# Queries and keys in three parts through the scratch, read in one or two transfers, with new first loads and new orders

## What is computed

```
Q = layernorm(x) @ Wq + bq                 # 8 x 128 x 512
K = context @ Wk + bk                      # 8 x 128 x 128
V = context @ Wv + bv
w = softmax(Q K^T / 4)                     # per head, 4 query heads share a key head
x = x + tanh(g_xattn) * ((w V) @ Wo + bo)
n = layernorm(x)
h = silu(n @ w1^T) * (n @ w3^T)            # 1792 features, block scales on w1, w3, w2
x = x + tanh(g_ffn) * (h @ w2^T)
```

## Time and profile before

| | |
|---|---|
| median of 3 runs | 391.2 us (389.21 to 392.38) |
| the profiled execution | 391.0 us, of which the span is 389.3 |
| TensorE busy | 371.2 us (95%) |
| VectorE, ScalarE, GpSimd busy | 253.6, 184.7, 154.9 us |
| moved by transfers | 34.96 MB, mean 90 GB/s |
| read from and written to device memory | 26.04 MB, 7.34 MB |

### The profile page before, as it was taken

One profiled execution on the slowest core, in us unless ns is written; L12 is line 12 of the kernel. 1 busy time (PEld: TensorE's weight loads), 2 busy tenths in 40 slices (PEclk: granted clock), 3 DMA queues, 4 the chain that ended last, 5 costly groups with the idle time before them and its releaser, 6 DMA issues.

```text
span 389.3 us, 6031 instructions
## 1 busy us (share of the span) xinstructions
PE 371.2 (95%) x2216; PEld 303.8 (78%) x2216; DVE 253.6 (65%) x411; ACT 184.7 (47%) x322; POOL 154.9 (40%) x134
## 2 busy tenths in 40 slices
PE   8979699989899999889999999999999999999996
PEld 6868589888677778668888888888888888888885
DVE  4666389979899976875767777443954344544434
ACT  3562389878889983622332422332332332432320
POOL 7534469989989987733333443000000000000000
PEclk9998699999999999989999999999999999999999
DMA  8979855767543500890000000000200000000002
GB/s 287 252 239 240 263 121 137 215 167 229 123 97 97 175 2 2 327 400 2 0 0 0 0 0 0 1 0 0 109 1 0 0 0 0 0 0 0 0 0 108
DMA packets 15604, 34.96 MB, mean 90 GB/s; under 512 B 2176, under 2 KB 7296, under 8 KB 14784
## 3 DMA queue, kind: packets, MB, share of 16 engines
q1 hardware_dynamic: 14864, 33.65, 28.9%
q10 hardware_dynamic: 720, 1.05, 0.8%
HBM read 26.04 MB, written 7.34 MB: 86 GB/s over the span
## 4 chain that ended last, share of the span: by engine, by line
PE 56%; DVE 1%; issue 0%
PE ps L1866 19%; PE ps L1868 19%; PE ps L1867 18%; DVE X L1317 1%; DVE hL L1339 0%
## 5 line engine op out<-in xcount | busy, mean ns | idle before, releaser
L1866 PE MATMUL ps<-x2HL,w13H 128*128 128x512 f32 x224 | 89.1, 398 | 0.0
L1868 PE MATMUL ps<-x2HL,w13L 128*128 128x512 f32 x224 | 88.5, 395 | 0.0
L1867 PE MATMUL ps<-x2HL,w13H 128*128 128x512 f32 x224 | 88.4, 394 | 0.0
L483 POOL TENSOR_TENSOR PL<-E,PH 128x512 f16<-128x512 f32 x64 | 74.1, 1178 | 10.2 <-ACT PH L784 7.9
L494 POOL TENSOR_TENSOR wres<-wres,gsc 128x1536 f32<-128x1536 f32 x14 | 42.0, 3006 | 48.7 <-DVE hf L1330 48.7
L803 ACT ACTIVATE T<-ps 128x512 f32<-128x512 f32 x28 | 16.7, 596 | 79.4 <-PE ps L1868 79.4
L1868 PEld LDWEIGHTS ps<-x2HL,w13L 128*128 128x128 f32 x224 | 42.0, 187 | 10.4
L1867 PEld LDWEIGHTS ps<-x2HL,w13H 128*128 128x128 f32 x224 | 42.0, 187 | 9.8
L1866 PEld LDWEIGHTS ps<-x2HL,w13H 128*128 128x128 f32 x224 | 42.0, 188 | 9.7
L1323 DVE SCALAR_TENSOR_TENSOR A<-T,ps 128x512 f32<-128x512 f32 x28 | 19.2, 685 | 46.0 <-ACT T L803 46.0
L1866 PE MATMUL ps<-w2H,hH 128*128 128x512 f32 x112 | 44.9, 401 | 2.7 <-DVE x2HL L1306 2.7
(11 more groups left out here) (102 smaller groups left out, 647.2 us busy)
## 6 DMA issues: line engine op xcount, KB each, us to landing
wres<-in_wff SPq DMA_DIRECT2D x14, 768.0 KB, 7.2
Qst<-qscr SPq DMA_DIRECT2D x21, 256.0 KB, 4.5
X<-in_x SPq DMA_DIRECT2D x8, 256.0 KB, 6.1
ct<-in_ctxt SPq DMA_DIRECT2D x6, 256.0 KB, 7.8
x2HL<-kscr SPq DMA_DIRECT2D x24, 64.0 KB, 3.5
qscr<-QTH SPq DMA_DIRECT2D x3, 512.0 KB, 4.3
qscr<-QTL SPq DMA_DIRECT2D x3, 512.0 KB, 3.7
out<-X SPq DMA_DIRECT2D x6, 256.0 KB, 2.1
```

Of the source, the lines that this page charges most:

```text
L483: pool.tensor_tensor(PL[:, g % NL, :], E[:, g % NE, :], PH[:, g, :], ALU.subtract).then_inc(pL_ok, 1)
L1866: pe.matmul(out_ap, aH, bH, start=start, stop=False)
L1867: pe.matmul(out_ap, aH, bL, start=False, stop=False)
L1868: return pe.matmul(out_ap, aL, bH, start=False, stop=stop)
```

## The change

It has five parts.

1. The scratch tensors get a third part. The query scratch holds high, high, low (parts 0, 1, 2), the key scratch high, low, high, just as the rows are stacked. So each pair writes queries three times and keys three times; the queries of a block come back in one read of 96 rows, the keys of a pair in two reads of 48 rows (every second row of 96). The order of features in the weights (`queries`, `keys`) is changed to match. A read waits for all three writes.
2. First loads: all are issued by SP, in the order key weights, context 0 and 1, x 0 and 1, value weights, biases, context 2, x 2, context 3, first half of the query weights. TensorE begins with keys and values in place of x. The select reads move behind the first queries, the out weights (1 MB) ahead of them.
3. `NWARM` is 12.
4. Some small work changes engine: the high half of the second query weights from VectorE to ScalarE, the first V part of all four pairs and the second of two pairs from ScalarE to VectorE, the first `clear_keys` from GpSimd to VectorE, one `max_rows` and two `q_high` from VectorE to ScalarE, two `shift` and two `shift2` from GpSimd to VectorE, one `epsilon2` the other way.
5. The lists of all engines are in a new order.

```
-NWARM = 16
+NWARM = 12
...
-        qscr = nc.dram_tensor("qscr", [NBATCH // 2, 2, 2, P, GJ * P], F32).ap()
-        kscr = nc.dram_tensor("kscr", [NBATCH // 2, 2, P, TWO], F32).ap()
+        qscr = nc.dram_tensor("qscr", [NBATCH // 2, 2, 3, P, GJ * P], F32).ap()
+        kscr = nc.dram_tensor("kscr", [NBATCH // 2, 3, P, TWO], F32).ap()
...
-        def keys_out(eng, p, low):
-            eng.dma_start(kscr[p, low], r32((KTL if low else KTH)[:])).then_inc((kh_out, kl_out)[low], 16)
-
-        def keys_in(eng, p, t, gg):
+        def keys_out(eng, p, t):
+            eng.dma_start(kscr[p, t], r32((KTL if t == 1 else KTH)[:])).then_inc((kh_out, kl_out, kg_out)[t], 16)
+
+        def keys_in(eng, p, gg):
             s = (NBATCH - NKST + 2 * p % NKST) * P
-            r = 32 * t + DH * gg
-            eng.dma_start(r32(kall(r, r + DH)[:, gg:KVH:2, s:s + TWO]),
-                         kscr[p, t % 2, 64 * gg:64 * gg + 64].rearrange("(r h) n -> r h n", h=PAIRS)).then_inc((k_in0, k_in1)[p % 2], 16)
+            eng.dma_start(r32(x2HL[gg:ROWS:2].rearrange("p a k n -> p (a k) n")[:, gg:KVH:2, s:s + TWO]),
+                         kscr[p].rearrange("t (d g h) n -> g (t d) h n", g=2, h=PAIRS)[gg]).then_inc((k_in0, k_in1)[p % 2], 16)
...
-        def queries_in(eng, n, t, done):
-            eng.dma_start(r32(Qst[32 * t:32 * t + 32, slot(n), :, :]).rearrange("r h n -> r (h n)"),
-                         qscr[n // 2, t // 2, n % 2].rearrange("(r h) n -> r (h n)", h=PAIRS)).then_inc(done, 16)
+        def queries_in(eng, n, done):
+            eng.dma_start(r32(Qst[0:ROWS, slot(n), :, :]).rearrange("r h n -> r (h n)"),
+                         qscr[n // 2, n % 2].rearrange("t (r h) n -> (t r) (h n)", h=PAIRS)).then_inc(done, 16)
...
+            sp.wait_ge(qg_out, 32)
+            sp.wait_ge(qh_out, 32)
+            sp.wait_ge(ql_out, 32)
+            queries_in(sp, 2, q_in0)
...
-            pe.wait_ge(k_in1, 96)
-            pe.wait_ge(q_in0, 48)
+            pe.wait_ge(k_in1, 32)
+            pe.wait_ge(q_in0, 16)
             scores(2, 0)
```

More of the change, by code:

```diff
@@ L351, in _ @@
             keys_out(sp, 2, 0)
-            sp.wait_ge(mrows, 2)
+            out_bias_in(sp)
+            queries_in(sp, 1, q_in2)
+            sp.wait_ge(sel_ok, 3)
+            select_rows(sp, 0)
+            select_rows(sp, 1)
+            keys_out(sp, 2, 2)
+            select_rows(sp, 2)
+            tokens_in(sp, 7)
+            select_rows(sp, 3)
+            sp.wait_ge(mrows, 1)
+            max_in(sp, 0, 0, 2)
+            sp.wait_ge(mrows, 2)
+            max_in(sp, 0, 2, 4)
+            sp.wait_ge(qT_H, 8)
@@ new lines, in _ @@
+            sp.wait_ge(qT_L, 12)
+            queries_out(sp, 2, 2, 0, 4, ql_out)
+            sp.wait_ge(mrows, 4)
+            max_in(sp, 2, 0, 4)
+            queries_out(sp, 2, 0, 0, 4, qh_out)
+            keys_out(sp, 3, 2)
+            sp.wait_ge(st_ps, 16)
+            keys_in(sp, 2, 1)
+            keys_in(sp, 2, 0)
+            sp.wait_ge(qg_out, 48)
+            sp.wait_ge(qh_out, 48)
+            sp.wait_ge(ql_out, 48)
+            queries_in(sp, 4, q_in2)
+            keys_out(sp, 3, 0)
@@ L1390, in _ @@
-            mean(3)
+            dve.wait_ge(vt_ps, 2)
+            v_first(2, W0)
+            dve.wait_ge(v1_ok, 2)
+            v_residue(2, W0)
             dve.wait_ge(qT_H, 3)
             q_low(W2, 2)
-            dve.wait_ge(mean1, 4)
+            statistics(5)
             epsilon(3)
-            v_residue(2, W0)
+            mean(4)
+            dve.wait_ge(qT_H, 4)
+            q_low(W1, 3)
+            v_third(2, W0)
             dve.wait_ge(rs1_ok, 4)
             shift(3)
-            dve.wait_ge(qT_H, 4)
@@ L1429, in _ @@
-            max_high(0, 2)
-            mean(5)
             dve.wait_ge(qT_H, 6)
-            q_low(W2, 1)
+            q_low(W0, 1)
             dve.wait_ge(s_ps, 4)
@@ L1480, in _ @@
             denominators(1)
+            mean(7)
             dve.wait_ge(den_ok, 2)
             sums(1)
-            dve.wait_ge(kT_H, 4)
-            k_low(W0)
+            dve.wait_ge(mean1, 8)
+            epsilon(7)
             dve.wait_ge(sum_ok, 2)
@@ L1524, in _ @@
             row_max(3, 0)
+            dve.wait_ge(den_ok, 5)
+            sums(0)
+            dve.wait_ge(xTH_ok, 7)
+            x_low(6, W2)
+            dve.wait_ge(sum_ok, 5)
+            divide(0)
+            dve.wait_ge(s_ps, 14)
+            row_max(3, 1)
             dve.wait_ge(pv_ps, 12)
@@ L2182, in _ @@
             scores_t(2, 4)
-            project_q(W2, 1, 0, 2)
+            project_q(W0, 1, 0, 2)
+            pe.wait_ge(k_in0, 64)
+            pe.wait_ge(max_ok, 16)
+            pe.wait_ge(q_in2, 32)
+            scores(4, 0)
             pe.wait_ge(E_ok, 20)
@@ L2266, in _ @@
             scores_t(4, 0)
+            pe.wait_ge(max_ok, 22)
+            scores(5, 2)
+            project(W2, DM, aTH, aTL, O0, 1)
+            pe.wait_ge(E_ok, 32)
+            scores_t(4, 1)
             pe.wait_ge(pL_ok, 29)
@@ L2301, in _ @@
-            pe.wait_ge(k_in1, 192)
-            pe.wait_ge(max_ok, 24)
-            pe.wait_ge(q_in1, 144)
-            scores(6, 0)
-            pe.wait_ge(mL_ok, 6)
-            turn_max(W1, 0, 4)
+            pe.wait_ge(E_ok, 37)
+            scores_t(4, 6)
+            turn4(W2, ON).then_inc(aT_ps, 1)
+            pe.wait_ge(max_ok, 25)
+            scores(6, 1)
+            pe.wait_ge(PH_ok, 38)
+            scores_t(4, 7)
+            pe.wait_ge(pL_ok, 35)
             pe.wait_ge(on_ok, 17)
@@ L2352, in _ @@
             turn_max(W2, 0, 4)
+            pe.wait_ge(on_ok, 19)
+            values(4, 6)
             pe.wait_ge(E_ok, 44)
             scores_t(5, 5)
+            values(4, 7)
+            turn4(W1, x2n).then_inc(x2T_ps, 1)
+            pe.wait_ge(max_ok, 29)
+            scores(7, 1)
+            pe.wait_ge(E_ok, 45)
+            scores_t(5, 6)
             pe.wait_ge(on_ok, 20)
             values(5, 0)
+            pe.wait_ge(pL_ok, 42)
             values(5, 1)
-            pe.wait_ge(mrows, 7)
```

1694 lines of the change are left out of this document (812 added, 882 removed).

## The result

The changed kernel takes 395.5 us (median of 20 runs, 390.3 to 400.4), the kernel before 391.7 beside it; the ratio is 1.009, with a 95% interval of 1.005 to 1.013. Forecast were 385 us and faster. In two later jobs (a job is one session on one chip, with the kernels in turn) the same changed kernel stood at 1.0114 (1.0035 to 1.0193; median 398.1) and 1.0188 (1.0136 to 1.0240; median 397.6) of the kernel before. Medians are over all executions; the ratios leave out those more than 1.5% above the fastest of their kernel, and the one profiled with the first measurement was such a one.

A forecast was written before the change was run, and what follows sets the result against it. The prediction took the first stage to hang on the DMA transfers, not on TensorE. Its terms, 3.4 + 1.3 + 1.5 = 6.2 us, taken from 391.1 gave 384.9, say 385 us, with a range of 380 to 394.

The forecast's parts named there:

- First term: First stage, up to the scores of block 2: gain of 3.4 us (3.0 + 1.4 - 1.0), from 0 to 6.
- the DMA work is through at 52.2: First stage: 2.1 us net transfer cost, less 1.95 us of idle time gone, after 52 us; landing at 54.0.
- The DMA share in 20 to 30: Sign of being right: the DMA engines' share in 20 to 30 us rises from 0.75 to 0.9.
- The scores of block 2 behind 57 us: Sign of being wrong: these scores start after 57 us, where 53 to 55 was forecast and 56.96 measured before.
- The wait at the door: Sign of being right: TensorE's wait before the feed-forward, 2.74 us at 166.94, falls below 2 us.
- price of an 8 KB packet: Sign of being right: 8 KB packets still cost 0.5 to 0.6 us of DMA engine time each.
- Second term: Key waits before the scores of blocks 4 and 6, 1.1 and 1.6 us: half gained, 1.3 us (0 to 2.7).
- Third term: Door of the feed-forward: a third of 4.4 us of wait and slow clock gained, 1.5 us (-1 to 4.4).
- work moved between engines: Mostly before 50 us: adds no instruction in sum; some 1 us for the largest piece if the cover fails.
- The transfers take it back: Rival, first stage: idle time stays 3.9 us, key packets 0.086; 388 to 390 us, within 1%; chance 0.28.
- One read waits for three writes: Rival, reads for blocks 4 and 6: TensorE stands 4 us or more at each; about 396 us; chance 0.14.
- port rule: Rival: each query read takes 1.2 us less, 3.6 us before block 2's scores; about 381 us; chance 0.08.

The follow-up runs named there:

- kernel with the queries first: Changed kernel, with second half of pair 1's queries and block 2's maxima transposes ahead of block 1's scores: 393.0 us (1.0039), again 394.9 us (1.0138).

## Why the prediction was wrong

**First term, 3.4 us of gain; measured a loss of about 1** (the table's 1.8 less the 0.9 of the warm-up). The step that failed is "so the DMA work is through at 52.2 [...] the scores of block 2 now start there, by waiting". The bill of the packets was right: I had 48.4 us of engine time before those scores. The windows give 0.89 x 20 + 9.9 + 10.7 + 6.3 = 44.7 up to 52, and the read of block 2, which hadn't begun, adds 96 packets of 8 KB at 0.54, 3.2 us: 47.9. But the engines' idle time didn't halve, from 3.9 to 1.95. It is 52 - 44.7 = 7.3 us, of which the first 2.5 us hold 2.0 (1.8 before), so it grew to 5.3; 3.7 of them lie in 42 to 52, most of it in 42 to 47, where SP waits for the second piece of the maxima and has the writes of pair 1's queries behind that. I read that all engines are full and took their sum for the bound. They are full up to about 43 us; from there the bound is the chain read, scores of block 1, second half of the queries of pair 1, write, read. And the kernel before reached these scores without a wait, so to start them by waiting at 54.0, with 1.4 us more done, TensorE had to save 4.4 us of what it lost before them. My sum had no term for that, and the waits ahead of blocks 0 and 1 went from 5.13 to 6.08 us. The rows for it were in front of me: the order in which these stand, and 3.38 us of wait ahead of block 1 in the earlier trace rows. The kernel with the queries first shows the chain: read and scores of block 2 move up by 4.6 and 2.5 us, no byte less moved.

**The signs.** The DMA share in 20 to 30 rose to 0.99, as said, and proved nothing, since it had only moved. The scores of block 2 behind 57 us was my sign of being wrong, and it came (59.39); the other, a wait for queries of 3 us or more at blocks 4 and 6, didn't (2.07 and none). The wait at the door (1.38 us) and the price of an 8 KB packet (0.50 us) were as said.

**Second term, 1.3 us, was right in its size and wrong in its sum.** Key waits fell from 2.7 us to 1.5. But a wait for queries of 2.07 us stands ahead of block 4, which the kernel before had for keys with 1.1. From 60 to 120 us the middle lost 2.3 more, it gained nothing: the waits for keys and queries went from 2.7 us to 3.6, and the mean clock from 1.00 to 0.94.

**Third term, 1.5 us: the gain is there, larger than I put it (lost in 160 to 190: 4.7 to 2.2), and the step that failed lies beside it.** I wrote that the new order "puts that scaling elsewhere" and didn't ask what else it puts elsewhere. The first product of the feed-forward had moved up, ahead of the values of block 6, and with it the same kind of VectorE operation into a run of GpSimd. It stood for 4.70 us. The stretch of 120 to 160 lost 5.5 us more, the largest piece of the miss, and my sum didn't have it at all: I costed "work moved between engines" only up to 50 us. That operation's place is shown to be only about 1 us of it (8.1 us lost, 6.9 with the product and the operation moved back); what takes the rest stays open.

**The rivals.** "The transfers take it back" came nearest in the first stage, for the wrong reason: idle time didn't stay at 3.9 us, it grew, and key packets did become cheaper. "One read waits for three writes" ended on the right side, but the three writes cost nothing in the old orders, and its sum was off: 11 us for 2.7 on 391.1, less the third term's 1.5, is 398, not 396. The gain of the port rule didn't come: three reads of 32 rows in 60 to 64 us gave 0.54 us a packet; in the changed kernel the window 60 to 64 holds one read of 96 rows.

```profile
DMA packets 93, 0.61 MB, mean 153 GB/s; under 512 B 14, under 2 KB 14, under 8 KB 20
...
q1 hardware_dynamic: 93, 0.61, 61.6%
```

61.6% of 64 us is 39.4; less about 1 us for the small ones and 6 packets of weights at some 0.3, 36.6 over 73 packets of 8 KB is 0.50 us each. By the rule of the Trainium skill ("SBUF — State Buffer", section on the DMA port swizzle), as I estimated from it, the wider read would have cost two thirds of the price, 0.36. It costs nine tenths. That doesn't refute the rule: the estimate took the three reads of 32 rows for served one after another, and they were issued within 1.25 us (from 59.78) and took 4.4 us each to land, so they may have overlapped. Key reads over 48 rows did become cheaper: in 101 to 104 us (second window below) 54.0% of 48 us is 25.9, less 23 packets of 8 KB at 0.54 leaves 13.5 over 208, 0.065 us each, where I had bounds of 0.086 and 0.047.

```profile
DMA packets 231, 0.39 MB, mean 128 GB/s; under 512 B 16, under 2 KB 208, under 8 KB 208
...
q1 hardware_dynamic: 231, 0.39, 54.0%
```

## What to carry to other kernels

When most engines are nearly full, don't take the sum of their work for the bound of a stage: write down the chain of issue, landing, product and next issue, and ask for each moved instruction what stands behind it in its queue. When a change brings a new order for every engine, go through the new lists to the end and put a price on each place where an instruction meets another neighbour; the part of the change with a name (the scratch) was worth nothing in the old orders, the rest (orders, first loads, work moved between engines) cost 1 to 2%. When you count lost time, leave out work that one of the kernels doesn't need. And a difference under 1% wants both kernels in one job: one kernel measured 0.9993 and 0.9894 in two.

## What the runs showed of the hardware

One VectorE operation with both inputs in SBUF, 1.2 us by itself (1024 elements a row), took 4.70, 2.21 and 1.44 us beside GpSimd, and one of 512 elements 3.24 and 2.64 instead of 0.68. At 130.67 it waited out three GpSimd operations in a row, 3.38 us from 130.91, and ended 1.08 us behind the last, which is about its own time. In the kernel before the pair falls out the other way:

```profile
132.26 3.27 POOL L483 TENSOR_TENSOR PL<-E,PH 128x512 f16<-128x512 f32 x2
...
133.06 1.44 DVE L1311 TENSOR_TENSOR w13L<-wres,w13H 128x1024 fp32r<-128x1024 f32 x1
```

Two GpSimd operations that take 2.29 us at 124.79 in the same kernel took 3.27, and VectorE's only 1.44. The second of the two stood:

```profile
133.45 2.08 POOL L483 TENSOR_TENSOR PL<-E,PH 128x512 f16<-128x512 f32 x1
```

So here VectorE got in between two GpSimd operations, and at 130.67 in the changed kernel it didn't, though two of them began behind its start (132.02 and 133.15). What decides that isn't shown. VectorE's operation with one input in PSUM kept its time beside GpSimd: 0.69 at 129.87, within GpSimd's run of 3.41 us from 127.32. The Trainium skill names the cause ("GPSIMD Engine Reference", section 1, Specifications): GpSimd's SBUF interfaces are shared with VectorE, and contention arises with VectorE instructions that have two SBUF inputs. The traces agree, and no run here takes one engine's operation away to prove it. What I hadn't expected is the length: VectorE can stand for a whole run of GpSimd's operations (three, 3.38 us), so such an operation must not stand ahead of anything that TensorE waits for.
